# First attention of a two-layer kernel: the next batch's gelu layer and first projections placed inside the batch tail

## The reference, cut to what matters

```python
x = x + L0_attn(L0_cond(x, side, side, w, u, cond), w_qkv, w_o, dw1, qkw, dd_w)

# L0_cond: sigmoid(x) * fac, where fac comes from forward and backward scans over
# the tokens of `side` (numerator and denominator, floored and inverted)
# L0_attn, on the conditioned input xc:
q, k, v = split(xc @ w_qkv)                       # q scaled by 16 ** -0.5
w = gelu(xc @ dw1) @ qkw                          # per token weights that mix heads
w1, w2 = split(w); w1 = rmsnorm(w1)
dd = tanh(xc @ dd_w)
logits = cross_head(q @ k.T, pre weights of w1, w2, dd)
probs  = softmax(where(causal, logits, min))
probs  = cross_head(probs, post weights of w1, w2, dd)
x_attn = (probs @ v) @ w_o.T
```

## Time and profile before

| | |
|---|---|
| time, median of 3 runs | 1254.99 us (1248.14 to 1258.76) |
| the profiled execution | 1248.21 us, its span 1246.3 us |
| busy in the span | PE 1007.3 us (81%), DVE 797.6 us (64%), ACT 605.0 us (49%), POOL 211.3 us (17%) |
| mean granted TensorE clock | 0.929 of 2.4 GHz |

### The profile page before, as it was taken

How to read it: one execution, slowest core, us unless ns; L and a number is a source line. 1 busy time by engine, 2 the same in 40 slices (tenths; PEclk the granted TensorE clock), 3 DMA queues, 4 the chain that set the end, 5 groups by cost and what they waited for, 6 DMA issues and landing times.

```text
span 1246.3 us, 18414 instructions
## 1 busy us (share of the span) xinstructions
PE 1007.3 (81%) x6320; PEld 717.5 (58%) x6320; DVE 797.6 (64%) x2038; ACT 605.0 (49%) x1454; POOL 211.3 (17%) x179
## 2 busy tenths in 40 slices
PE   0788878887788878869698888888898857999995
PEld 0667666665676667654265655633333344887884
DVE  4568876887677787857347888547667550554442
ACT  3178716881677257833143333136566721454442
POOL 1001020102010201014513333200000003223222
PEclk9989988998899989978899999969999965999998
DMA  9999300000000000023348887514555508477772
GB/s 269 236 233 233 79 1 1 2 1 1 1 2 1 1 1 1 1 95 106 105 145 278 269 290 224 203 44 169 194 202 179 218 18 300 144 223 228 210 242 28
DMA packets 74876, 161.28 MB, mean 129 GB/s; under 512 B 10642, under 2 KB 56990, under 8 KB 70432
## 3 DMA queue, kind: packets, MB, share of 16 engines
q1 hardware_dynamic: 65904, 145.52, 38.3%
q0 software_dynamic: 8880, 14.60, 4.5%
HBM read 127.68 MB, written 62.62 MB: 153 GB/s over the span
## 4 chain that ended last, share of the span: by engine, by line
PE 44%; DVE 19%; DMA 14%; ACT 12%; issue 6%; POOL 2%; another core or an unknown queue 1%; SPq 1%; ACTq 0%; POOLq 0%; DVEq 0%
PE ps L1504 41%; DMA out<-arena 7%; ACT arena L596 3%; DMA arena<-in_w0all 3%; DMA made<-arena 2%; DVE arena L1008 2%; DVE arena L1337 2%; ACT arena L581 2%; POOL out L507 2%; ACT arena L574 1%; DVE arena L1032 1%; ACT arena L589 1%; DVE arena L977 1%; PE ps L1910 1%
## 5 line engine op out<-in xcount | busy, mean ns | idle before, releaser
L1504 PE MATMUL ps<-arena 128*128 128x256 f16 (+15 forms) x4712 | 790.2, 343 | 98.9 <-ACT arena L589 31.5
L1504 PEld LDWEIGHTS ps<-arena 128*128 128x128 f32 (+8 forms) x4712 | 538.4, 151 | 277.5 <-issue 113.9
L1488 DVE CAST arena<-arena 128x256 f16<-128x256 f32 x120 | 36.8, 307 | 110.4 <-ACT arena L782 109.9
L1337 DVE TENSOR_REDUCE arena<-ps 128x4 f16<-128x1024 f32 (+1 forms) x48 | 58.8, 1227 | 51.5 <-PE ps L1504 51.5
L448 POOL TENSOR_TENSOR den<-den,backd 128x512 f32<-128x512 f32 x9 | 11.4, 1268 | 453.5 <-DVE euv L880 453.5
L782 ACT ACTIVATE arena<-ps,arena 128x256 f32<-128x256 f32 x120 | 55.8, 475 | 58.1 <-PE ps L1504 57.0
L1032 DVE SCALAR_TENSOR_TENSOR arena<-arena 128x128 f32<-128x128 f32 x240 | 83.6, 409 | 0.6
L999 DVE SCALAR_TENSOR_TENSOR arena<-arena,ps 128x128 f32<-128x128 f32 (+1 forms) x128 | 47.2, 410 | 56.9 <-PE ps L1504 39.0
L596 ACT ACTIVATE arena<-ident,arena 128x128 f32<-128x128 f32 x256 | 80.9, 387 | 0.0
L477 POOL DMA_INDIRECT made<-arena x47 | 53.0, 1129 | 115.2 <-DVE arena L1250 111.6
L507 POOL DMA_INDIRECT out<-arena x30 | 47.1, 1571 | 146.0 <-DMA out<-arena 85.6
(11 more groups left out here) (282 smaller groups left out, 1296.5 us busy)
## 6 DMA issues: line engine op xcount, KB each, us to landing
arena<-split SPq DMA_DIRECT2D x15, 2048.0 KB
arena<-in_w0all SPq DMA_DIRECT2D x47, 608.0 KB
slots<-in_blank SPq DMA_DIRECT2D x17, 1040.0 KB, 16.4
arena<-in_w1all SPq DMA_DIRECT2D x16, 1024.0 KB, 6.7
split<-arena SPq DMA_DIRECT2D x32, 512.0 KB, 3.6
slots<-in_blank SPq DMA_DIRECT2D x9, 1072.0 KB, 19.1
arena<-slots SPq DMA_DIRECT2D x47, 130.0 KB, 3.2
arena<-slots SPq DMA_DIRECT2D x15, 268.0 KB
```

Of the source, the lines that this page charges most:

```text
L1337: dve.tensor_reduce(out, ps[:, at:at + 2].rearrange("p j (r s) -> p j r s", r=nr), X, ALU.max, negate=True).then_inc(max1_done, 1)
L1504: return pe.matmul(o, l, r, start=start, stop=stop, skip_group_check=shared)
```

## The change

- PE: the hidden layer of batch b+1 goes between the last tail product and the turn of `o_tok` of batch b, and writes banks 6 and 7 instead of 4 and 5. The first half of the tokens of b+1 goes between that turn and the output projection. Mixing and the second half follow the projection. Batch 0 has its own hidden layer and first half in front.
- ACT: the copy of `oT` (`outputs_turned`) is now ACT's, behind the gelus of the next batch. The sigmoid of batch b+2 is taken at the end of the tail of batch b, that of batch 1 behind the tanh of batch 0, and the two that nothing used are gone. `exp_slice(2b+1)` goes from pass 0 to pass 1.
- DVE: the residual add of batch b (`residual_first`) goes behind the first scaled q and k of batch b+1. The value stacks go behind the copies of the turned stacks. The steps of both slices move: `split[6:9]` between the rank copies, `split[9:11]` ahead of the loop, `split[11]` and all of `own` into the loop, the last three of them and `condition_batch(b+1)` into pass 8, ahead of `mix`.

```diff
@@ scalar
             def sigmoid_batch(b):
+                if b:
+                    act.wait_ge(xc_ready, b)
                 act.activation(sig[:], xT[:, :, bass.ds(b * T, T)], ACT.Sigmoid).then_inc(sig_ready, 1)
+            def outputs_turned(b):
+                act.wait_ge(tail_pe, b * TAIL0 + 8)
+                act.activation(oT.rearrange("p a t -> p (a t)"), ps[:, 3], ACT.Copy).then_inc(tail_act, 1)
...
-                    act.activation(hid[:, 2 * h:2 * h + 2].rearrange("p c t -> p (c t)"), ps[:, 4 + h],
+                    act.activation(hid[:, 2 * h:2 * h + 2].rearrange("p c t -> p (c t)"), ps[:, 6 + h],
                                    ACT.Gelu_apprx_tanh).then_inc(evac_a, 1)
+                if b:
+                    outputs_turned(b - 1)
...
+                if b == 0:
+                    sigmoid_batch(1)
...
-                    if p == 0:
+                    if p == 1:
                         exp_slice(2 * b + 1)
-                sigmoid_batch((b + 1) & (B - 1))
...
                 exp_slice(2 * b + 2)
+                if b + 2 < B:
+                    sigmoid_batch(b + 2)
+            outputs_turned(B - 1)
@@ vector
+            def residual_first(b):
+                dve.wait_ge(tail_pe, b * TAIL0 + 9)
+                here = xT[:, :, b * T:(b + 1) * T]
+                st.tell(dve.tensor_tensor(here, here, ps[:, 7].rearrange("p (m t) -> p m t", m=CT), ALU.add),
+                        x_done, b + 1)
...
                 scaled_qk(0, 1)
-                for step in split[6:9]:
-                    step()
+                if b:
+                    residual_first(b - 1)
...
                 scaled_qk(1, 3)
-                for step in split[9:10]:
-                    step()
...
+                for u in range(1, 10, 2):
+                    dve.wait_ge(projected, b * PROJ0 + 8 + u)
+                    st.tell(dve.tensor_copy(turned(u), turned_bank(u)), evac_d, b * EVD0 + 4 + u // 2)
                 for tt in range(TT):
                     v = heads(v0[:, tt])
...
-                for u in range(1, 10, 2):
-                    dve.wait_ge(projected, b * PROJ0 + 8 + u)
-                    st.tell(dve.tensor_copy(turned(u), turned_bank(u)), evac_d, b * EVD0 + 4 + u // 2)
-                for step in split[10:12]:
-                    step()
...
-                own = slice_steps(2 * b + 1, 2 * b + 1)
-                for step in own[0:2]:
+                for step in split[6:9]:
                     step()
...
-                extra = {0: own[3:4], 1: own[4:5], 2: own[5:6], 4: own[6:8], 5: own[8:9], 6: own[9:10], 7: own[10:12]}
+                own = slice_steps(2 * b + 1, 2 * b + 1)
+                extra = {0: split[11:12] + own[0:1], 1: own[1:2], 2: own[2:3], 3: own[3:4], 4: own[4:5], 5: own[5:6],
+                         7: own[6:9]}
...
-                for step in own[2:3]:
+                for step in split[9:11]:
                     step()
...
+                    if p == N0 // 2:
+                        for step in own[9:12]:
+                            step()
+                        if b + 1 < B:
+                            condition_batch(b + 1, 0, b + 2)
...
-                condition_batch((b + 1) & (B - 1), 0, b + 2)
...
-                dve.wait_ge(tail_pe, b * TAIL0 + 8)
-                st.tell(dve.tensor_copy(oT.rearrange("p a t -> p (a t)"), ps[:, 3]), tail_dve, b * 4 + 4)
                 for step in split[4:6]:
                     step()
-                dve.wait_ge(tail_pe, b * TAIL0 + 9)
-                here = xT[:, :, bass.ds(b * T, T)]
-                st.tell(dve.tensor_tensor(here, here, ps[:, 7].rearrange("p (m t) -> p m t", m=CT), ALU.add),
-                        x_done, b + 1)
-
+            residual_first(B - 1)
@@ tensor
+            for b in range(B):
+                if b == 0:
+                    hidden0(b)
+                    tokens0(b, 0)
+                mixing0(b)
+                tokens0(b, 1)
...
                 ins.then_inc(tail_pe, 1)
+                if b + 1 < B:
+                    hidden0(b + 1)
-                pe.wait_ge(tail_dve, b * 4 + 3)
+                pe.wait_ge(tail_dve, b * 3 + 3)
                 for k in range(CT):
                     for tt in range(TT):
                         ins = pe.transpose(ps[:, 3, (k * TT + tt) * P:(k * TT + tt + 1) * P],
                                            o_tok[:, tt, k * P:(k + 1) * P], ident[:])
                 ins.then_inc(tail_pe, 1)
-                pe.wait_ge(tail_dve, b * 4 + 4)
+                if b + 1 < B:
+                    tokens0(b + 1, 0)
+                    pe.wait_ge(evac_a, (b + 1) * EVA0 + 2)
+                pe.wait_ge(tail_act, b * 6 + 6)
                 for m in range(CT):
                     for k in range(CT):
                         ins = mm(ps[:, 7, m * T:(m + 1) * T], wo0[:, k, m * P:(m + 1) * P], oT[:, k], k == 0, k == CT - 1)
```

More of the change, by code:

```diff
@@ L1069, in _ @@
                         step()
-                condition_batch((b + 1) & (B - 1), 0, b + 2)
                 for i in range(2):
                     dve.wait_ge(tail_pe, b * TAIL0 + 1 + i)
-                    st.tell(dve.tensor_copy(mixqT[:, i], ps[:, i, 0:384]), tail_dve, b * 4 + 1 + i)
+                    st.tell(dve.tensor_copy(mixqT[:, i], ps[:, i, 0:384]), tail_dve, b * 3 + 1 + i)
                 split = slice_steps(2 * b + 2, 2 * b + 2)
@@ L1098, in _ @@
                     if tt:
[L1099 removed]
+                        st.tell(ins, tail_dve, b * 3 + 3)
                     else:
                         st(ins)
[L1102 to L1103 removed]
                 for step in split[4:6]:
                     step()
[L1106 to L1109 removed]
+            residual_first(B - 1)
             def condition_all(which, act_done, done):
@@ L1507, in _ @@
             pe.wait_ge(ld["attn0"], 128)
-            for b in range(B):
+            def hidden0(b):
                 pe.wait_ge(xc_ready, b + 1)
+                if b:
+                    pe.wait_ge(tail_act, (b - 1) * 6 + 2)
                 for c in range(4):
                     for k in range(CT):
-                        ins = mm(ps[:, 4 + c // 2, (c % 2) * T:(c % 2 + 1) * T], dw1[:, k, c * P:(c + 1) * P],
+                        ins = mm(ps[:, 6 + c // 2, (c % 2) * T:(c % 2 + 1) * T], dw1[:, k, c * P:(c + 1) * P],
                                  xc[:, k], k == 0, k == CT - 1)
@@ L1516, in _, with tokens0 @@
                         ins.then_inc(projected, 1)
-                for tt in range(TT):
-                    tok = slice(tt * P, (tt + 1) * P)
-                    for o, w in ((ps[:, 2 * tt], wqkv[:, :, 0:2 * C]), (ps[:, 2 * tt + 1, 0:C], wqkv[:, :, 2 * C:]),
-                                 (ps[:, 2 * tt + 1, C:C + 64], ddw)):
-                        for k in range(CT):
-                            ins = mm(o, xc[:, k, tok], w[:, k], k == 0, k == CT - 1)
-                        if w is not ddw and w.shape[2] == C:
-                            continue
-                        ins.then_inc(projected, 1)
-                    if tt == 0:
-                        pe.wait_ge(evac_a, b * EVA0 + 2)
-                        for t2 in range(TT):
-                            for c in range(4):
-                                ins = mm(ps[:, 6, t2 * 256 + c * 64:t2 * 256 + (c + 1) * 64],
-                                         hid[:, c, t2 * P:(t2 + 1) * P], qkw[:, c])
-                        ins.then_inc(projected, 1)
+            def tokens0(b, tt):
+                tok = slice(tt * P, (tt + 1) * P)
+                for o, w in ((ps[:, 2 * tt], wqkv[:, :, 0:2 * C]), (ps[:, 2 * tt + 1, 0:C], wqkv[:, :, 2 * C:]),
+                             (ps[:, 2 * tt + 1, C:C + 64], ddw)):
+                    for k in range(CT):
+                        ins = mm(o, xc[:, k, tok], w[:, k], k == 0, k == CT - 1)
+                    if w is not ddw and w.shape[2] == C:
+                        continue
+                    ins.then_inc(projected, 1)
+            def mixing0(b):
+                pe.wait_ge(evac_a, b * EVA0 + 2)
+                for t2 in range(TT):
+                    for c in range(4):
+                        ins = mm(ps[:, 6, t2 * 256 + c * 64:t2 * 256 + (c + 1) * 64],
+                                 hid[:, c, t2 * P:(t2 + 1) * P], qkw[:, c])
+                ins.then_inc(projected, 1)
+            for b in range(B):
[4 more added lines that the diff above has]
+                tokens0(b, 1)
                 for u in range(10):
```

9 lines of the change are left out of this document (4 added, 5 removed).

## The result

| | before | after |
|---|---|---|
| time, median of 4 runs | 1255.4 us (1248.1 to 1258.8) | 1212.3 us (1209.8 to 1214.0) |
| ratio, 95% interval | | 0.968 (0.965 to 0.971) |
| the profiled execution | 1248.2 us, span 1246.3 | 1209.8 us, span 1208.0 |
| mean granted TensorE clock | 0.929 | 0.939 |

The change makes the kernel 3.2% faster. I had forecast 1228 us (1214 to 1246), a gain of 27 us on the profiled execution; that gain is 38.4. The medians differ by 43.1, since the profiled execution of the kernel before was 7.1 under its median and that of the changed kernel 2.5. Direction and mechanism were right, and the time lies 2 us under the range.

A forecast was written before the change was run, and what follows sets the result against it. No engine bounds alone; hand-overs do. Boundaries 13.5 plus rank products 9.1 make 22.6, plus 4.4 of clock is 27: 1221 from the profiled 1248.2, or 1228 against the median 1255; range 1214 to 1246.

The forecast's parts named there:

- The rank products: Before each batch's rank products: value stacks behind DVE's five copies start them 2.3 us earlier, 9.1 over four batches.
- The boundary: Between batches, last o_tok sum to ACT's v0 copy: 16.23 us falls to 11.7, gain 4.5, times three 13.5.
- late mixing: Last pass of the head loop: DVE's added steps delay mixing the last heads, making o_tok about 0.7 us late.
- overhang: At the boundary: PE's hidden layer ends 0.55 us after DVE's o_tok is ready, delaying the turn behind it.
- The loop: Inside the head loop: scans, floor, exp and POOL's sums shift between passes, with no change in time taken.
- POOL's sums: Head loop, moved from behind pass 2 to behind pass 5: no change; bounds 1.84 us saved or lost again per batch.
- The clock: Slow PE pieces at boundaries and rank products: up to 6.2 us more gain at full clock, 4.4 of it taken.
- my first rival: Slow clock comes back elsewhere: three pieces of 3.2 us each return, 17 of 27 remain, 1238 us; chance 0.15.
- The steps do not move into a new wait: Rival: DVE's longer list or POOL's sums arrive last, costing 7 to 9 us over four batches, 1236; chance 0.10.
- the hidden layer ran at 1.00 and held the turn: Rival at the boundary: hidden layer at low clock delays the turn, 3.2 us more each, 9.5 in all, 1238; chance 0.05.
- the residual's wait: DVE behind the boundary: residual add waits for the output projection ahead of mixw's copy; 0.69 us, said to fit.
- All slow pieces of the forecast: Rival by the clock page: all 6.2 us of slow pieces go, gain 28.8, 1226 us, within the forecast case.

The follow-up runs named there:

- the filler run: Kernel before plus eight unread products on PE between the last tail product and the turn of o_tok: 1233.4 us, ratio 0.997.
- two filled holes per batch: Changed kernel plus two spare products in each of PE's two gaps in pass 1 and again in pass 8: 1188.8 us, ratio 0.960.

## Why the prediction was right, and where its sum was short

**The rank products** (forecast 9.1 and the clock): exact. The copies end at 170.7, the products start at 170.86, and the stretch lost 2.27 us at equal clock. DVE's longer list did not become the last: no batch waits for rankkT. The clock there came though PE still waits for the copies right ahead of the products:

```profile
163.84 5.20 PE L1574 MATMUL ps<-ident,arena 128*128 128x128 f32 x40 [1.86 <-DVE arena L970]
170.86 5.47 PE L1519 MATMUL ps<-arena 128*128 128x128 f32 x32 [1.83 <-DVE arena L985]
```

The prediction said "with the wait gone". This wait was 1.82 us before and is 1.83 now (0.88 in the third batch). What is gone is the other one, up to 2.23 us ahead of the last turn, whose 40 pieces now run in one row.

**The boundary** (forecast 11.7 us, with 0.70 of late mixing and 0.55 of overhang): this is the step that was mis-sized. Measured are 10.27 from o_tok on, and o_tok itself came 0.36 late, so 10.6. The overhang is 0.12 instead of 0.55 (0.48 behind the slow last pass of the second batch) and the way from turn to tokens 0.44 instead of 0.71 (151.86 to 152.30). The late mixing did delay mixq's turn by 0.6 (it starts 4.96 us behind ACT's last turned copies, 4.36 before), but the tail products started 7.34 behind them, against 7.33, and the run with the mixing first showed that it is worth nothing. My main error was to add the late o_tok of DVE (0.70) and the overhang of PE (0.55), which run side by side, where only the later counts: together they are 0.48. The step is worth 3.3 us of the 11.4 by which the forecast was short.

**The loop, taken as free of gain,** gave 4.4 at equal clock. 2.1 are exp of the slice out of pass 0, which I had priced at 0.61 in either pass; ACT's turned copies come 0.52 us earlier without it, and in the second pass it delays nothing that the marks show. 2.3 are POOL's sums. I had read the stall rightly, 1.84 per batch, but assumed the same price at the new place. In pass 6 the four sums hit one pair of maxima and cost 1.24, since they start at 115.65 and half of them are over before the pair begins.

**The clock** (forecast 4.4 of up to 6.2): measured 6.6. The ranks gave 4.4, the second and third boundary 1.7, pass 1 1.8; the last pass, tail and boundary of the second batch took 1.3 back, net of what the third batch's last pass had lost before (15.79). That the low clock would come back elsewhere was my first rival, and it is right as a mechanism: 17.11 us in that pass, and nearly the whole of the filler run. Why the toll stayed small here, no run shows; my reading is that the change removed idle time of PE and the filler run only padded it.

**The rest** (1.5 us behind the attention) I did not explain. With it the gaps of 3.3, 4.4 and 2.2, less 0.2 behind the last o_tok, make up the 11.4 within 0.2.

**The range.** Its low end doesn't follow from the terms it names. The profile less 28.8 is 1219.4; less POOL's stall of 1.84 once it is 1217.6, and less the stall once per batch, 1212.0. I wrote 1214. What took the time under it is in none of its terms: 3.3 us at the boundaries, 2.1 of exp, and 1.5 behind the attention.

**The other rivals.** The steps do not move into a new wait; the hidden layer ran at 1.00 and held the turn by 0.12 us, 0.48 in the second batch; the residual's wait held nobody (2.28 us idle, then 1.04 more until mixw). The Trainium skill ("TensorE: Matmul & The Clock Gate", The HAM clock gate) says that the reduced clock is the resting state and activity lifts it. All slow pieces of the forecast did go, as by that rule, and the fillers raised the clock with work that nobody reads. The sum by it would have been 28.8, still short, since the boundary and the loop were too.

## What to carry to other kernels

When independent work is moved into a wait of TensorE, price the work twice: as time taken off the chain, and as clock for everything behind the wait. Compare the streams of both engines at the next point where they meet and count only the later one; do not add the delays of each. If the low clock comes and goes with such holes, fill the next hole as well, with spare products if nothing useful is at hand, since filling one alone may give part or all of the gain back in a slow stretch elsewhere.

## What the runs showed of the chip that I had not expected

The clock is a matter of the whole sequence. One filled hole gained 5.1 us and lost 5.7 elsewhere; two filled holes per batch behind a dense boundary gained 11.0 us at the last residual, and the steps from pass 1 to pass 2 then agreed to 0.02 us in three batches (10.67 to 10.69) where they had spread from 12.2 to 13.6.

VectorE's maximum over two SBUF inputs took 0.94 to 1.48 us while POOL added beside it and 0.28 and 0.42 when it did not, but the residual add (one input from SBUF, one from PSUM) kept its 0.69 us at 157.26 under POOL's sums at 156.29 and 157.52; at 164.75 in the run with the hidden layer behind the projection, where POOL is idle, it took 0.68. The Trainium skill ("SBUF — State Buffer", Who interferes with whom) says that a VectorE instruction with two SBUF inputs contends with GpSimd's reads and one with at most one such input does not; the rows agree.

Two chips gave the changed kernel 1212.3 and 1201.9 us with an attention that is 1.2 us longer on the second. What lies behind it, where the DMA traffic is, is 11.7 us shorter there; no run here separates the cause.
